# Second sparse layer's first four feature chunks placed between the last attention batch's output products; row statistics behind the normalising; the sparse input's transpose evacuated ahead of the exponentials in four tiles

## The reference, cut to what matters

```python
x = x + _L0_ffn_ref(_layernorm(x), ...)      # first sparse layer
x = x + _L0_attn_b_ref(_layernorm(x), ...)   # attention
x = x + _L0_ffn_ref(_layernorm(x), ...)      # second sparse layer

# inside the sparse layer
xc = einsum('ngf,gf->ng', x.reshape(n, g, 4), conv_w) + conv_b   # features
mean, var = mean(xc, axis=0), mean((xc - mean) ** 2, axis=0)     # over ALL 4096 rows
xa = gelu((xc - mean) * rsqrt(var + eps) * gamma + beta)
score = softmax(xa @ lin_w.T + lin_b)
s_v, s_i = top_k(score, 32)      # once for outputs, once for inputs
```

## Time and profile before

| | us |
|---|---|
| median of 3 runs | 1357.16 |
| lowest, highest | 1355.29, 1364.52 |
| the profiled execution | 1359.22 |
| its span, first to last instruction | 1357.5 |
| busy in the span: PE, DVE, ACT, POOL | 1222.2, 1147.6, 1052.3, 954.4 |
| mean granted TensorE clock | 0.974 |

### The profile page before, as it was taken

How to read it: one execution, slowest core, us unless ns; L and a number is a source line. 1 busy time by engine, 2 the same in 40 slices (tenths; PEclk the granted TensorE clock), 3 DMA queues, 4 the chain that set the end, 5 groups by cost and what they waited for, 6 DMA issues and landing times.

```text
span 1357.5 us, 30767 instructions
## 1 busy us (share of the span) xinstructions
PE 1222.2 (90%) x10252; PEld 751.2 (55%) x10252; DVE 1147.6 (85%) x3124; ACT 1052.3 (78%) x2347; POOL 954.4 (70%) x1098
## 2 busy tenths in 40 slices
PE   5999999688888889999999999999999999677776
PEld 2555554345445546666666666666666666344443
DVE  7999996797999988888777788877878854899998
ACT  3323424786999889999999989999999985877776
POOL 4367553486787777777776777777777773488887
PEclk9999999996999999999999999999999999898988
DMA  6200000100002000010000000000000000000000
GB/s 153 61 1 1 0 0 1 42 1 1 24 28 77 30 20 24 24 25 25 25 25 2 2 2 2 2 2 3 2 2 2 2 2 1 1 31 17 32 17 31
DMA packets 35529, 25.32 MB, mean 19 GB/s; under 512 B 16358, under 2 KB 32044, under 8 KB 35372
## 3 DMA queue, kind: packets, MB, share of 16 engines
q1 hardware_dynamic: 35372, 23.36, 6.1%
HBM read 14.89 MB, written 8.39 MB: 17 GB/s over the span
## 4 chain that ended last, share of the span: by engine, by line
PE 45%; ACT 12%; issue 11%; DVE 9%; POOL 4%; DVEq 0%; DMA 0%; ACTq 0%; POOLq 0%; SPq 0%
PE banks L2123 7%; PE banks L2125 7%; PE banks L2111 6%; PE banks L2064 4%; PE banks L2140 4%; PE banks L2141 4%; DVE arena L1595 4%; PE banks L2142 4%; ACT arena L1218 3%; DVE arena L1590 3%; ACT arena L1230 2%; PE banks L2040 2%; ACT arena L1066 2%; PE banks L2186 1%; PE banks L1987 1%
## 5 line engine op out<-in xcount | busy, mean ns | idle before, releaser
L877 POOL TENSOR_TENSOR arena<-arena 128x512 f16<-128x512 f32 x383 | 437.5, 1161 | 145.1 <-ACT arena L1230 141.3
L1218 ACT ACTIVATE arena<-banks 128x512 f32<-128x512 f32 x512 | 302.6, 599 | 41.8 <-PE banks L2125 37.4
L1674 DVE TENSOR_REDUCE arena<-banks 128x1 f32<-128x512 f32 x512 | 326.3, 680 | 4.8 <-PE banks L2111 2.6
L1230 ACT ACTIVATE arena<-arena 128x512 f16<-128x512 f32 x512 | 315.6, 631 | 0.0
L2140 PE MATMUL banks<-arena 128*128 128x65 f16 x2016 | 211.4, 193 | 1.0
L2141 PE MATMUL banks<-arena 128*128 128x64 f16 x2016 | 211.6, 195 | 0.0
L2142 PE MATMUL banks<-arena 128*128 128x65 f16 x2016 | 210.6, 193 | 0.0
L1700 DVE TENSOR_TENSOR arena<-arena 128x512 f16<-128x512 f32 x129 | 107.5, 834 | 121.4 <-ACT arena L1230 121.2
L1590 DVE MAX8 arena<-arena 128x8 f32<-128x256 f32 x512 | 190.0, 412 | 23.8 <-issue 13.7
L1595 DVE MATCH_REPLACE8 arena<-arena 128x256 f32<-128x256 f32 x512 | 205.7, 409 | 0.9 <-issue 0.4
L2140 PEld LDWEIGHTS banks<-arena 128*128 128x128 f16 x2016 | 187.9, 96 | 31.7 <-issue 9.9
(11 more groups left out here) (241 smaller groups left out, 2591.7 us busy)
## 6 DMA issues: line engine op xcount, KB each, us to landing
arena<-q_store SPq DMA_DIRECT2D x48, 128.0 KB, 2.7
x<-in_L_attn_a_x SPq DMA_DIRECT2D x8, 512.0 KB, 3.9
q_store<-arena SPq DMA_DIRECT2D x32, 128.0 KB, 1.8
out<-x SPq DMA_DIRECT2D x7, 512.0 KB, 2.9
arena<-arena SPq DMA_DIRECT2D x64, 1.0 KB, 1.9
arena<-in_L_attn_a_W_in SPq DMA_DIRECT2D x1, 768.0 KB, 5.8
arena<-in_L_attn_a_W_mid SPq DMA_DIRECT2D x1, 512.0 KB, 7.4
arena<-in_L_attn_a_w_w SPq DMA_DIRECT2D x2, 256.0 KB, 7.7
```

Of the source, the lines that this page charges most:

```text
L877: nc.gpsimd.tensor_tensor(pr_lo[c][:, kt, :], pr[:, kt, :], pr_hi[c][:, kt, :], ALU.subtract).then_inc(a_lP, 1)
L1218: nc.scalar.activation(pr[:, kt, :], ps[6 + kt % 2][:, :], ACT.Exp, scale=SM_SCALE).then_inc(a_P, 1)
L1230: nc.scalar.activation(pr_hi[c][:, kt, :], pr[:, kt, :], ACT.Copy).then_inc(a_hi, 1)
L1674: nc.vector.tensor_reduce(mx_half[c][:, i // 2, i % 2:i % 2 + 1], ps[bank][:, :], X, ALU.max).then_inc(a_mx, 1)
```

## The change

Three parts.

1. The second layer's features of chunks 0 to 3 (`SECOND_EARLY = 4`) are made between the last batch's output products: PE does one chunk's `feature_chunk` and the next chunk's transposes behind an output product for j = 1 to 4, the transposes of chunk 0 come ahead of the first `out_turn`, and chunks 4 to 7 follow behind the last product. ACT, POOL and DVE are reordered to match. PSUM banks change: the transposes go to banks 6 and 7 (0 and 1 for chunks 5 and 7), the output products from 6 and 7 to 2 and 3. The last chunk's statistics are made tile by tile as its rows come.
2. Statistics of an output chunk that stood ahead of `normalise` come behind it: at w = 0 of batches 2 and 3, and behind the last item.
3. In tiles 6, 10, 14 and 18 of the first sparse layer ACT copies the transposed sparse input (`ffn_sT`) ahead of `ffn_exp`, not behind it.

```diff
@@ constants
+        SECOND_EARLY = 4
+        def second_bank(n):
+            return 0 if n in (NCH - 3, NCH - 1) else 6
@@ POOL: n over the chunks
                 if n == 2:
                     rstd_of("out", NCH - 3)
+                if n == NCH - 2:
                     rstd_of("out", NCH - 2)
-                if n == 4:
+                if n == NCH - 1:
                     rstd_of("out", NCH - 1)
@@ ACT: ffn, tiles
                     ffn_zT(f, t + 2, q)
+                    if f == 0 and t in HEAD_STATS_AT:
+                        ffn_sT(f, t, q)
                     ffn_exp(f, t + 1, 1 - q)
-                    ffn_sT(f, t, q)
+                    if f or t not in HEAD_STATS_AT:
+                        ffn_sT(f, t, q)
@@ ACT: behind the last item (the old loop at the head of ffn(1) is gone)
+            second_rows(0)
+            second_rows(1)
+            second_turned(0)
             for j in range(FINALS):
                 out_turned((BATCH - 1) * FINALS + j, j % 2)
+                if 1 <= j <= SECOND_EARLY:
+                    second_rows(j + 1)
+                    second_turned(j)
+            second_rows(NCH - 2)
+            second_turned(NCH - 3)
+            second_turned(NCH - 2)
+            second_rows(NCH - 1)
+            second_turned(NCH - 1)
@@ DVE: in the items
                         if what == "out_final":
-                            final(n, bank)
+                            final(n, bank, () if w == 0 else (0, 1, 2))
...
                 if W:
                     normalise(W - 1)
-            final((BATCH - 1) * FINALS - 1, 4)
+                if w == 0 and B > 1:
+                    dve.wait_ge(a_fx, (B - 1) * FINALS)
+                    stats_of("out", 2 * B - 3)
+            final((BATCH - 1) * FINALS - 1, 4, ())
+            dve.wait_ge(a_O, (ALL - 1) * 2)
             normalise(ALL - 1)
+            dve.wait_ge(a_fx, (BATCH - 1) * FINALS)
+            stats_of("out", NCH - 3)
             for j in range(FINALS):
-                final((BATCH - 1) * FINALS + j, 6 + j % 2)
+                J = (BATCH - 1) * FINALS + j
+                final(J, 2 + j % 2, (0, 1, 2) if j < TPC else ())
+                if j < SECOND_EARLY:
+                    features(1, j)
+                if j >= TPC:
+                    dve.wait_ge(a_fx, J + 1)
+                    dve.sem_inc(s_turn, 1)
+                    nc.vector.bn_stats(nst6[:, J % TPC, :], x[:, J, :]).then_inc(n_c, 1)
+            stats_of("out", NCH - 1, (1, 2))
@@ PE: behind the last item (the old loop at the head of ffn(1) is gone)
+            def second_turn(n):
+                pe.wait_ge(s_zh, 3 + n)
+                if n == 0:
+                    pe.wait_ge(a_P, ALL * KT)
+                if n == NCH - 3:
+                    pe.wait_ge(a_fe, NT)
+                transposes(LN_FFN2 + n, z_rows[n % 2], second_bank(n))
+            second_turn(0)
             for j in range(FINALS + 1):
                 J = (BATCH - 1) * FINALS + j
                 ...
                         out_final(J - 1, 2 + (j - 1) % 2, half)
+                if 1 <= j <= SECOND_EARLY:
+                    feature_chunk(1, j - 1)
+                    second_turn(j)
+            second_turn(SECOND_EARLY + 1)
+            for n in range(SECOND_EARLY, NCH):
+                feature_chunk(1, n)
+                if n + 2 < NCH:
+                    second_turn(n + 2)
```

More of the change, by code:

```diff
@@ L1099, in ffn @@
             def ffn(f):
[L1100 to L1113, removed]
                 for p in range(2):
@@ L1298, in _, with second_rows, second_turned @@
                 high(W, KT - 1)
+            def second_rows(n):
+                act.wait_ge(n_p, 4 * group_of["out", n] + 4)
+                z_rows_of(n, z_rows[n % 2], 2)
+            def second_turned(n):
+                zT_chunk(LN_FFN2 + n, n % 2, second_bank(n))
+            second_rows(0)
+            second_rows(1)
+            second_turned(0)
             for j in range(FINALS):
                 out_turned((BATCH - 1) * FINALS + j, j % 2)
+                if 1 <= j <= SECOND_EARLY:
[6 more added lines that the diff above has]
+            second_turned(NCH - 1)
             ffn(1)
@@ L1619, in ffn @@
                 if f:
-                    for n in range(NCH):
+                    for n in range(SECOND_EARLY, NCH):
                         features(f, n)
@@ L1658, in query_low, with final @@
                                             ALU.subtract).then_inc(a_ql, 1)
-            def final(J, bank):
+            def final(J, bank, part=(0, 1, 2)):
                 dve.wait_ge(a_fm, J + 1)
                 nc.vector.tensor_tensor(x[:, J, :], x[:, J, :], ps[bank][:, 0:D], ALU.add).then_inc(a_fx, 1)
-                if J % TPC == TPC - 1:
+                if J % TPC == TPC - 1 and part:
                     dve.wait_ge(a_fx, J + 1)
-                    stats_of("out", J // TPC)
+                    stats_of("out", J // TPC, part)
             def largest_of(W, i):
@@ L1828, in feature_chunk @@
                 pe.wait_ge(s_zT, ((LN_FFN2 if f else LN_FFN1) + n) * 2 + 2)
+                if f and n == 0:
+                    pe.wait_ge(a_fx, (BATCH - 1) * FINALS)
                 if n > (1 if f else 4):
@@ L1995, in ffn @@
                     feature_chunk(0, NCH - 1)
[L1996 to L2004, removed]
                 for p in range(2):
@@ L2247, in _ @@
                     for half in range(2):
-                        out_final(J - 1, 6 + (j - 1) % 2, half)
+                        out_final(J - 1, 2 + (j - 1) % 2, half)
+                if 1 <= j <= SECOND_EARLY:
+                    feature_chunk(1, j - 1)
+                    second_turn(j)
+            second_turn(SECOND_EARLY + 1)
+            for n in range(SECOND_EARLY, NCH):
+                feature_chunk(1, n)
+                if n + 2 < NCH:
+                    second_turn(n + 2)
             ffn(1)
```

## The result

| | before | after |
|---|---|---|
| median of 20 runs each, us | 1356.17 | 1363.8 |
| lowest, highest | 1353.67, 1364.52 | 1362.21, 1366.5 |
| ratio after / before, 95% interval | | 1.0054 [1.0043, 1.0065] |
| the profiled execution | 1359.22 | 1365.93 |
| its span | 1357.5 | 1364.2 |

The changed kernel is 7.6 us slower: within 1% of before, but clearly on the slow side, and above the range that ended at 1362.5. Of the runs behind the experiments' tables three lie far above all others (1380.18 us of parts_1_2, 1469.22 of tile_6, 3158.81 of the kernel before), and the ratios leave them out.

The account below looks back on a forecast made before the run. PE bounds attention and the stretch behind its last item; DVE bounds the first sparse layer's tiles except where logits come late. Terms -0.85 - 0.4 - 2.0 + 3.3 = 0.05 us, from the median 1357.2 us, range 1352.0 to 1362.5.

Parts of the forecast that it names:

- Part 3, tile 6: First sparse layer: PE goes on 1.24 us earlier, the clock falls later, DVE waits less; -2.0 us, bounds 0 and -6.05.
- 1.62 + 4.43 becomes 4.0: DVE's waits ahead of tiles 9 and 10 in the profiled execution, together 6.05 us, shrink to 4.0.
- a rule by which the clock should return soon: Skill's rule that sustained activity restores full clock within a few us; set aside because the trace showed 0.50 through 18 us.
- Part 3, tiles 10, 14 and 18: First sparse layer: ACT stands for PE's transposes, +0.85, +1.22 and +1.22 us; term +3.3, bounds 0 and +4.5.
- Rival C: First layer: ACT's new stands make PE stand and the clock fall; one fall 1360.2 us, two 1363; chance 0.25.
- The sum: Whole kernel: -0.85 - 0.4 - 2.0 + 3.3 = 0.05 us, taken from the median: 1357.2.
- Part 1: Behind the last attention item: -0.9 chunk 0's transposes, -0.65 earlier normalise, +0.7 chunk 7 exposed; -0.85 us, bounds -1.55 and +1.0.
- Nothing else should wait inside the loop: Output product loop: a turn is 4.2 us of PE, in which each other engine has one chunk and one tile.
- Part 2: Attention item 32: PE's 1.66 us wait for normalise goes, the next row maximum limits the gain; -0.4 us; item 48: 0.
- Rival B: Tiles 6 to 9: slow clock gone, DVE regains both waits, 6.05 us in place of 2.0; 1353.2 us; chance 0.2.
- Rival D: Tiles 10, 14 and 18: the edits cost nothing, the chain being ahead of DVE; 1353.9 us; chance 0.1.
- The range: Whole kernel: 1352.0 to 1362.5 us, taking in rivals B, C with one to two falls, and run spread; leaving out 0.2.

Follow-up runs that it names:

- parts_1_2: The changed kernel with ACT's copy behind the exponentials again in every tile, so without part 3: 1354.87 us against 1355.98 before, ratio 0.9989.
- tile_6: The kernel before with ACT's copy of the transposed sparse input first in tile 6 alone: 1360.0 us against 1355.98 before, ratio 1.0031.
- before_again: The kernel before, unchanged, profiled a second time: 1352.56 us in that execution.
- before_busy: The kernel before with six spare PE products in tile 6 and ten in tile 7: 1352.66 us against 1354.56 before, ratio 0.9987.
- changed_busy: The changed kernel with 10, 8 and 4 spare PE products in tiles 7, 11 and 19: 1361.98 us against 1354.56 before, ratio 1.0055.
- parts_1_2_busy: Parts 1 and 2 without part 3, plus six spare PE products in tile 6 and ten in tile 7: 1353.54 us against 1356.64 before, ratio 0.9981.
- early_3_rows: parts_1_2_busy with three early chunks, not four, and ACT's half of chunk 7's rows ahead of its chunk 6 copy: 1354.04 us, ratio 0.9981.
- tile_6_busy: The kernel before with the copy first in tile 6 alone and ten spare PE products in tile 7: 1357.14 us against 1356.64 before, ratio 0.9997.
- changed_busy_2: The changed kernel with 13, 10, 4 spare PE products in tiles 7, 11, 19 and five each in 14 and 18: 1357.8 us against 1355.33 before.

## Why the prediction was wrong, point by point

**Part 3, tile 6: this step failed, in sign.** "From there on tile 7 and 8 go as before but 1.95 us earlier ... 1.62 + 4.43 becomes 4.0. Term -2.0." The 4.0 was right (3.84 in the changed kernel, 4.05 in tile_6). The 6.05 from which it was subtracted was not the kernel's usual state but one profiled execution, 2.06 us above the median of its three runs and 3.05 above that of twenty, whose slow stretch lasted 24 us where before_again's lasted 7. The sum then took the -2.0 from the median, as if all runs had paid the 6.05. Against before_again the term is +3.8, and by the medians of tile_6 and before +4.0. I had both warnings at hand: the profiled execution stood above its median, and a rule by which the clock should return soon. There the prediction used the Trainium skill (TensorE: Matmul & The Clock Gate, What's actually happening: sustained activity releases the throttle) and set it aside since the trace disagreed. The 18 us of the earlier trace rows, 24 in the whole trace, do disagree with it; the 7 us of before_again are much nearer. I weighed it as a rule for both kernels alike, and didn't see that an early return takes away most of the cost of the fall at 310 (0.6 us left) but not of one at 317 to 320 (3.2 left).

**Part 3, tiles 10, 14 and 18.** "Term +3.3": ACT stands 0.73, 1.13 and 1.13 us for 0.85, 1.22 and 1.22, and the delays at full clock are 0.5 + 1.2 + 1.1 = 2.8. Mechanism right, size nearly. The 2.8 isn't all: the sum counted the clock's falls elsewhere at nothing. In the changed kernel they cost 2.8 in tile 11 (delay from tile 12 to 14 is 3.2, less the 0.5 of the stand) and 1.7 in tile 19. This is the second step that failed. Rival C had it, at 3 us each, in the right place in tile 11 (POOL's input, 2.24 us) and near it behind tile 18; its two falls gave 1363, the measured median is 1363.8. That the number came so near is in part luck: it holds the -2.0 for tile 6, which was wrong by some 6, and 3 us for the fall that cost 1.7. As a mechanism it got 0.25, and should have been in the forecast: the kernel before fell after a wait of 1.67 us, and the edit itself made two new waits of 1.42 us and lengthened the one of tile 11 from 1.01 to 2.24.

**The sum.** By the trace against before_again: +3.3 by tile 10, stands 2.8, falls 2.8 + 1.7, together 10.6 of the 10.7 measured; less 0.8 for parts 1 and 2. The two whole executions lie 13.4 us apart (1365.93 and 1352.56): these 9.9, 1.66 ahead of tile 0 and 1.85 in the second layer's tiles and behind them. The medians show 7.6: before_again lies 3.6 below the median of its kernel, and the profiled execution of the changed one 2.1 above its own. In how many executions before pays for slow stretches wasn't measured.

**Part 1.** Forecast -0.85, measured -0.52. The statistics behind `normalise`: PE's first output turn is at 1126.53, 0.58 earlier against the preceding addition than 1121.30 was (forecast 0.65, with chunk 0's transposes ahead of it as forecast). The piece less on the chain and the new wait nearly cancel: from that turn to the last aggregate 35.99 us before and 36.05 after. The wait was 0.90 for 0.7, and of the releaser only half was seen: POOL's `rs` is complete at 1156.21, but ACT comes free for its half of the rows at 1156.34, behind its copy of chunk 6. "Nothing else should wait inside the loop" held within 0.1.

**Part 2.** Forecast -0.4 at item 32, measured -0.31, for the reason given: the wait of 1.66 went and 1.07 came back for the next maximum. Item 48 gave nothing that can be seen.

**Rival B** (slow clock gone, 1353.2) didn't come in the changed kernel. before_busy is its state reached by other means, and gives 1352.66 against 1354.56. **Rival D** falls with the steps of 1.2 and 1.1 us in changed_busy, at full clock.

**The range** ended at C with two falls from a base in which tile 6 was a gain. There were three falls, one of them where I had put the gain. The prediction also held that a measurement of this kernel tells nothing under 1%; the interval of the ratio, 1.0043 to 1.0065, tells 0.5%.

The best kernels of the study are parts_1_2_busy (0.9981 [0.9966, 0.9997]), the only one whose interval stays below 1, early_3_rows (0.9981 [0.996, 1.0001]) and before_busy (0.9987 [0.9972, 1.0003]): by the traces parts 1 and 2 are worth 0.8 to 1.0 us, and part 3 only costs.

## What to carry to other kernels

Before you price a stall that comes with a slow clock, find out whether it is there in most executions: a profiled run above its own median is one draw, and a second profile costs little. An edit that shortens one wait of PE can move the idle time to PE's next wait, as here from tile 6 (1.67 to 0.47 us) to tile 7 (3.04); ask what work a slow clock would cover there. On an engine that works strictly in order, move an instruction ahead only where its input is ready: in three of the four tiles here it wasn't, and the others behind it were.

## What the runs showed of the hardware that I had not expected

- A fall of the clock in the same kernel and place, behind waits of 1.67 and 1.68 us, lasted 7 us in one execution and 24 in another, with PE busy 6.00 of 6 and 11.43 of 12 us in the long one. What decides between them isn't settled.
- The price of a slow stretch goes by its place as well as by its length. At tile 10, against the -0.6 of the traces at full clock, 7 us from 310 cost 0.6, 24 us from 310 6.2, 7 us from 320 3.2, and 10 us from 318 4.4 (tile_6).
- The clock can fall behind short waits: in tile 19 of the changed kernel behind 1.42 and 0.95 us, five us apart; in tile_6_busy behind one of 0.88 in one execution and not behind 0.87 in the other; in tile 11 behind 0.84 and 1.06 in three kernels with spare products in tiles 6 and 7, and not in before_busy.
- A few spare products ahead of PE's waits (37 of them in five tiles of changed_busy_2) kept the clock at 1.00 through 200 us, and with them the changed kernel's median lies 2.5 us above that of before, where it lay 7.6 above without (each against the runs of before beside it).
